# Causal attention: the row maxima are subtracted on GpSimd, and the exponential of a unit is one ScalarE instruction

## What is computed

```python
slopes = 2.0 ** (-8.0 * h / 16)                      # h = 1..16
bias   = where(pos_q >= pos_k, -slopes[h] * |pos_q - pos_k|, -inf)
s      = q @ k.T * 8 ** -0.5 + bias                  # [heads, 128, 128] of one sequence
attn   = softmax(s, axis=-1)
x      = layernorm(x + (attn @ v) @ Wo.T + bo)
```

## Time and profile before

| | |
|---|---|
| median of three runs | 2991.36 us (2991.24 to 2993.08) |
| span of the profiled execution, first to last instruction | 3015.3 us |
| causal stage in it | about 1480 to 2030 us |
| one pair of the causal stage in its steady part | 16.60 us |
| busy in such a pair: TensorE, ScalarE, VectorE, GpSimd | 15.48, 15.29, 14.39, 5.63 us |

### The profile page before, as it was taken

How to read it: one execution, slowest core, us unless ns; L and a number is a source line. 1 busy time by engine, 2 the same in 40 slices (tenths; PEclk the granted TensorE clock), 3 DMA queues, 4 the chain that set the end, 5 groups by cost and what they waited for, 6 DMA issues and landing times. The chain is left out here.

```text
span 3015.3 us, 69304 instructions
## 1 busy us (share of the span) xinstructions
PE 2737.1 (91%) x21504; PEld 1982.6 (66%) x21504; DVE 1805.1 (60%) x5293; ACT 2070.9 (69%) x7235; POOL 1460.1 (48%) x1978
## 2 busy tenths in 40 slices
PE   8999999999999956998799999978999999699987
PEld 6666777777777746998355555546776666458874
DVE  6883344443444444554688888876677776444545
ACT  6766778777787743443699999976888888522224
POOL 3442224444444454555433333325678887724665
PEclk9999999999999987999899999998999999799998
DMA  9910030220400402221310000000000010001225
GB/s 264 338 47 15 19 116 16 80 78 20 129 27 20 135 30 72 73 70 57 115 56 10 9 10 8 10 22 10 13 27 28 29 31 17 29 26 56 80 79 185
DMA packets 179960, 185.08 MB, mean 61 GB/s; under 512 B 32844, under 2 KB 168537, under 8 KB 179216
## 3 DMA queue, kind: packets, MB, share of 16 engines
q1 hardware_dynamic: 162032, 145.14, 16.1%
q0 software_dynamic: 17280, 34.13, 3.4%
q10 hardware_dynamic: 288, 1.38, 0.2%
HBM read 58.34 MB, written 111.48 MB: 56 GB/s over the span
## 5 line engine op out<-in xcount | busy, mean ns | idle before, releaser
L678 POOL TENSOR_TENSOR wide_probs<-wide_exps,wide_inv_sum 128x308 f32<-128x308 f32 x256 | 179.3, 700 | 488.9 <-DVE wide_inv_sum L1409 486.0
L1400 DVE TENSOR_REDUCE wide_neg_max<-banks 128x4 f32<-128x308 f32 x256 | 122.5, 478 | 473.6 <-PE banks L982 448.9
L1116 ACT ACTIVATE causal_exps<-causal_biased,causal_neg_max 128x128 f32<-128x128 f32 x1024 | 325.8, 391 | 31.1 <-DVE causal_neg_max L1400 29.7
L1119 ACT ACTIVATE wide_exps<-banks,wide_neg_max 128x77 f32<-128x77 f32 x1024 | 315.8, 326 | 0.3 <-DVE wide_neg_max L1400 0.2
L658 POOL DMA_INDIRECT sorted_x<-send,place_i x240 | 244.9, 1020 | 96.0 <-issue 40.5
L1116 ACT ACTIVATE rotary_exps<-banks,rotary_neg_max 128x77 f32<-128x77 f32 x1024 | 252.0, 351 | 15.1 <-DVE rotary_neg_max L1400 13.7
L1103 ACT ACTIVATE wide_probsT<-banks 77x512 f32<-77x512 f32 x256 | 152.1, 594 | 153.6 <-PE banks L991 149.5
L1656 ACT ACTIVATE gelu_hidden<-banks,gelu_slot 128x256 f32<-128x256 f32 x284 | 116.7, 471 | 157.3 <-PE banks L1833 153.1
L1587 POOL DMA_INDIRECT results<-swiglu_tile_out,swiglu_dest_i x142 | 147.7, 1040 | 141.2 <-DVE swiglu_tile_out L1738 97.8
L1119 ACT ACTIVATION_READ_ACCUMULATOR wide_exps<-banks,wide_neg_max 128x1 f32 x1024 | 213.9, 209 | 0.0
L1587 POOL DMA_INDIRECT results<-gelu_tile_out,gelu_dest_i x142 | 140.8, 991 | 142.3 <-DVE gelu_tile_out L1743 119.0
(11 more groups left out here) (382 smaller groups left out, 7339.3 us busy)
## 6 DMA issues: line engine op xcount, KB each, us to landing
sorted_x<-blank SPq DMA_DIRECT2D x1, 34848.0 KB, 116.8
sorted_x<-blank SPq DMA_DIRECT2D x4, 8712.0 KB, 30.3
gelu_tile_in<-sorted_x SPq DMA_DIRECT2D x71, 132.0 KB
swiglu_tile_in<-sorted_x SPq DMA_DIRECT2D x71, 132.0 KB
gelu_back<-results SPq DMA_DIRECT2D x16, 512.0 KB, 7.7
swiglu_back<-results SPq DMA_DIRECT2D x16, 512.0 KB, 6.2
X<-in_x SPq DMA_DIRECT2D x8, 512.0 KB, 7.3
regions<-in_g_w SPq DMA_DIRECT2D x2, 2048.0 KB, 20.9
```

The source lines that it names most:

```text
L678: pool.tensor_tensor(probs[:, m % SLOTS], exps[:, m % SLOTS], inv_sum[:, m % SLOTS].unsqueeze(2).to_broadcast([P, HU, NK]), ALU.mult).then ...
L1116: last = act.activation(exps[:, (NU * c.c + k) % ES, h], scores[:, h * NK:(h + 1) * NK], ACT.Exp, bias=neg_max[:, k % SLOTS, h:h + 1])
L1119: last = act.activation(exps[:, k % SLOTS, h], scores[:, h * NK:(h + 1) * NK], ACT.Exp, bias=neg_max[:, k % SLOTS, h:h + 1], accum_out=exp ...
L1400: dve.tensor_reduce(neg_max[:, k % SLOTS], scores.rearrange("p (h n) -> p h n", h=HU), AX.X, ALU.max, negate=True).then_inc(max_done, 1)
```

## The change

On GpSimd a new function `take_max` runs at every k of pair `c`, behind the keys and ahead of the inverse root and the residual. It waits for the unit's `neg_max` and for its slot of `exps` to be free, adds the four negated maxima, each spread over 128 columns, to the slot of `biased`, and writes the sum to the slot of `exps`. A new semaphore, `lessened`, counts it. ScalarE waits for `lessened` instead of `max_done` and takes one exponential of 512 columns in place. VectorE's waits for a free slot of `biased` and of `neg_max` go to `lessened` instead of `exps_done`.

```diff
+            def take_max(c, k):
+                pool.wait_ge(max_done, c.count(NU, k + 1))
+                if before(c, k, ES) is not None:
+                    bc, bk = before(c, k, ES)
+                    pool.wait_ge(probsT_ps, bc.count(NU, bk + 1))
+                pool.tensor_tensor(exps[:, (NU * c.c + k) % ES], biased[:, k % BS].rearrange("p (h n) -> p h n", h=HU),
+                                   neg_max[:, k % SLOTS].unsqueeze(2).to_broadcast([P, HU, NK]), ALU.add).then_inc(lessened, 1)
...
                     if kind != "wide":
                         keys_ahead(pool, f, c, k, POOL_KEYS)
+                    if kind == "causal" and c is not None:
+                        take_max(c, k)
...
-                    if c is not None:
+                    if c is not None and kind == "causal":
+                        act.wait_ge(lessened, c.count(NU, k + 1))
+                        e_slot = exps[:, (NU * c.c + k) % ES]
+                        act.activation(e_slot, e_slot, ACT.Exp).then_inc(exps_done, 1)
+                    elif c is not None:
...
-                    dve.wait_ge(exps_done, bc.count(NU, bk + 1))
+                    dve.wait_ge(lessened, bc.count(NU, bk + 1))
...
-                            dve.wait_ge(exps_done, bc.count(NU, bk + 1))
+                            dve.wait_ge(lessened if kind == "causal" else exps_done, bc.count(NU, bk + 1))
```

More of the change, by code:

```diff
@@ L530, in softmax_attention @@
             sem(n) for n in ("s_ps", "max_done", "exps_done", "inv_done", "probs_done"))
-        biased_done, after_done = sem("biased_done"), sem("after_done")
+        biased_done, after_done, lessened = sem("biased_done"), sem("after_done"), sem("lessened")
         back_ps, inv_total_done, norm_done, oT_ps, oT_done = (sem(n) for n in ("back_ps", "inv_total_done", "norm_done", "oT_ps", "oT_done"))
@@ L1107, in step @@
                         front(f, k, 0)
-                    if c is not None:
+                    if c is not None and kind == "causal":
[3 more added lines that the diff above has]
+                    elif c is not None:
                         act.wait_ge(max_done, c.count(NU, k + 1))
-                        scores = biased[:, k % BS] if kind == "causal" else s_bank[k % 2]
+                        scores = s_bank[k % 2]
                         if before(c, k, ES) is not None:
```

## The result

The changed kernel takes 3076.73 us (3075.89 to 3080.68), the kernel before 2992.22 in the same comparison; the ratio is 1.0287, with a 95% interval from 1.0273 to 1.0302. The forecast was slower, 3048 us; the loss is 84.5 us instead of 57, at the upper edge of the range.

What follows compares the result with a forecast made beforehand. One unit's latency through VectorE and ScalarE was taken to close the causal pair's loop; a pair goes from 16.60 to 18.44 us, 30 x 1.84 + 2 = 57 us on 2991.4, giving 3048 us, range 3003 to 3078.

Steps and rivals of the forecast that it cites:

- The prices of the addition, the exponential: GpSimd's addition of 128x512 was put at 1.05 us, ScalarE's exponential of 512 columns at 0.64.
- the queue in front of unit 3: On GpSimd, unit 2's addition, inverse root and keys precede unit 3's addition; its transposes start at 11.94 instead of 10.69.
- VectorE's additions for units 6 and 7: End of pair, after the last score matmul: expected to start some 0.26 us late instead of 0.12, at 14.27.
- S01: Score matmul of units 0 and 1, which starts a pair; the next was forecast at 18.44 us instead of 16.60.
- the first two pairs: Start of the causal stage: no inverse root in GpSimd's queue, so about half the loss, 2 us counted.
- The 161 us for ScalarE: Less ScalarE time from shorter exponentials, 256 x 0.63 us; counts only where a chain ends in it.
- the sentence on TensorE's clock: TensorE's busy share falls to 84%; its clock stood at 1.00 at 90%, so nothing was counted for it.
- a slower GpSimd: Rival: additions of 1.26 us and slower handovers cost 2.77 us a pair, 86 us; 3077 us, 12%.
- S67: Score matmul of units 6 and 7, behind unit 3's transposes; forecast at 12.88 instead of 11.63 us, 1.25 later.
- the wait for the inverse root: VectorE's first write of X waits until 9.17, ends near 10.3; unit 4's maximum near 12.2, judged off the path.
- TensorE runs free: Rival: GpSimd's part hidden, TensorE loses its 1.12 us idle a pair, 36 us in all; 2955 us, 8%.
- only the end of the pair pays: Rival: GpSimd's queue is covered and a pair loses 0.45 us, 14 us in all; 3006 us, 12%.

Runs made afterwards that it cites:

- the first experiment: Changed kernel with four unread 128x128 matmuls on TensorE ahead of the second turned output, in its wait; 3047.94 us, ratio 1.0185.
- the version with four exponentials: Changed kernel, GpSimd's addition kept, with four ScalarE exponentials of 128 columns without bias column instead of one of 512; 3067.62 us, ratio 1.0261.
- the third experiment: Changed kernel with GpSimd's addition ahead of the masked keys in each step instead of behind them; 3069.74 us, ratio 1.0261.
- ScalarE's half alone: Changed kernel without GpSimd's addition and its semaphore; one 512-column exponential reads the biased scores, maxima not subtracted; 2957.06 us, ratio 0.9881.

## Why the prediction was wrong, point by point

**The direction and the prices were right.** A pair at full clock takes 18.43 us where 18.44 was summed, and the first experiment, which holds the clock, gives 3047.94 us for 3048. The prices of the addition, the exponential and the queue in front of unit 3 were each within 0.02 us. The agreement is better than its parts, and that is luck. VectorE's additions for units 6 and 7 start 0.14 late and not 0.26; from the turned output to S01 are 0.35 instead of 0.23, since the clock has begun to fall there (0.55 in that stretch), so that with the clock held the pair takes 18.30 and loses 1.70 us, not 1.84. And the first two pairs, for which 2 us in all were counted, lose 2.64 and 2.15 in the first experiment (18.02 and 18.68 us for 15.38 and 16.53). One error takes back most of the other. The 161 us for ScalarE count each exponential at its full length, though one starts before the other has ended; by busy time they are some 145.

**The step that failed** is the sentence on TensorE's clock: it "stood at 1.00 at 90%, and I count nothing for it". A busy share of 40 us in another stage was taken for the condition, and the loss by the clock was put at nothing. In the changed kernel the full-clock pair has 16.02 of 18.43 us busy, 87%, not far from that row, and the clock falls; in the version with four exponentials it is 15.98 of 18.76, 85%, and the clock stays up. So the share does not decide by itself. By the pairs the fall costs (1.32 + 1.40) / 3 = 0.91 us each, over 31 pairs 28 us, which is the difference of the first experiment and of the forecast alike. The prediction named the fall only as a thing that would make the loss larger, with no price and no chance; it should have been a rival, priced by the matmul that comes right behind the wait: 2.08 - 1.13 = 0.95 us, some 30 us if every pair is hit. The range's upper end came from a slower GpSimd, which did not occur; the measured time came to its edge for another reason.

**The path.** The sum came to VectorE's additions for units 6 and 7 through GpSimd's queue, unit 3 and S67, and the wait for the inverse root was set aside: "late, but unit 4 is transposed only behind S67". That was too easy. In the changed kernel VectorE is busy almost without a break from the write of X that waits for the inverse root to those additions, and they start at 14.12; behind S67 they could have started at 14.01 (its end at 13.98 and the 0.03 seen with four exponentials). So the inverse root's chain ends last, by 0.11 us, and the third experiment, which brings S67 0.94 us forward, leaves them at 14.12. The summed time was near because the two chains happen to be nearly equal; that they are was not known.

**The rivals.** TensorE runs free (2955 us) is what ScalarE's half alone does, 2957 us, so the condition on the addition was the right one. That only the end of the pair pays did not come to pass: TensorE waits 0.68 us for unit 3 in the pair shown, and with the clock held a pair loses 1.70 us, not 0.45. The addition took 1.04 us and not the 1.26 of the slower rival.

**What stays open.** Why two of three pairs begin at the lower level and not all, and why the clock stays up in other pairs behind a longer wait: 1.34 us where the version with four exponentials settles, 1.36 in the pair shown of the third experiment. So the length of one wait does not decide by itself either. The runs show that filling the wait or taking it away brings the clock back, and that a longer wait without GpSimd's work brings it down more often; they don't show the rule.

## What to carry to other kernels

An engine with idle time is no free place for a step if the step is put into the chain that closes the loop: there its latency counts, with all that stands in front of it in that engine's queue. Find that chain first and look for what can be moved past it; here one small copy moved in ScalarE's order is worth 30 us. And where a change makes TensorE wait longer, give the fall of its clock a price of its own, from the matmuls that come right behind the wait.

## What the runs showed of the hardware

- TensorE's granted clock fell to 0.50 behind a wait of 1.17 us in a stage in which it is some 87% busy, in two of three pairs, and a score matmul then took 2.08 us instead of 1.13; behind 1.04 us in the kernel before it did not, and neither did it in some pairs of other versions behind 1.34 and 1.36 us.
- Matmuls that nobody reads, 1.16 us a pair, put into that wait, saved 29 us; in the kernel before with a delayed copy, twice as many of them saved 65 us.
- Four exponentials of 128 columns with a column of biases take 1.27 us, without it 0.91, one of 512 without it 0.63: more than half of what ScalarE saves comes from the bias column, not from merging four instructions.
